# A graph network on one core: features before weights on one queue, digits of keys stored once, sixteen folded products ahead of the tail

## The reference

```
h = relu(layernorm(x));  x = x + attention(h, src, dst, W, a)         # softmax of scores over the edges of a node
h = relu(layernorm(x));  x = x + convolutions(h, [src,dst], W, b)     # three layers with self loops
h = relu(layernorm(x));  x = x + recurrent(h, [src,dst], W, GRU, MLP) # five steps
h = relu(layernorm(x));  x = x + weighted(h, src, dst, edge_weight, W1, b1, W2, b2)
```

## Time and profile before

| | us |
|---|---|
| median of 3 runs | 2409.83 |
| lowest and highest | 2408.52, 2412.48 |
| the profiled execution, whole | 2413.03 |
| its span (first to last instruction) | 2411.2 |
| prepare, until the barrier lets VectorE on | 105.8 |
| counts, until the scatter list is stored | about 199 |

### The profile page before, as it was taken

The page is one execution under the profiler, slowest core; times in us unless marked ns, Lnnn a source line. Parts: engine busy times, 40 slices in busy tenths (PEclk is TensorE's granted clock), DMA queues, the critical chain, the costliest instruction groups (busy, mean ns, idle before and its releaser), DMA issues.

```text
span 2411.2 us, 27684 instructions
## 1 busy us (share of the span) xinstructions
PE 2187.6 (91%) x9986; PEld 1206.7 (50%) x9987; DVE 1036.4 (43%) x2909; ACT 772.6 (32%) x1403; POOL 627.7 (26%) x434
## 2 busy tenths in 40 slices
PE   5599978998859996898999999999999999998998
PEld 4244467555525444354445554555445544464444
DVE  6699979998935457233112212122122111112202
ACT  3377767887823333222111111111111111112200
POOL 2000000000014433343444344443443344441000
PEclk9799955999979998899999999999999999999999
DMA  5200072444421112333222322223122322135582
GB/s 174 91 10 11 8 242 83 138 145 144 155 54 1 1 32 46 86 61 74 47 30 46 67 38 37 41 41 85 22 35 45 73 33 30 22 62 179 210 304 97
DMA packets 182305, 186.96 MB, mean 78 GB/s; under 512 B 105144, under 2 KB 168794, under 8 KB 178103
## 3 DMA queue, kind: packets, MB, share of 16 engines
q1 hardware_dynamic: 115288, 137.83, 18.2%
q0 software_dynamic: 56784, 1.28, 7.1%
q10 hardware_dynamic: 10106, 46.19, 5.3%
HBM read 100.85 MB, written 84.41 MB: 77 GB/s over the span
## 4 chain that ended last, share of the span: by engine, by line
PE 54%; DMA 3%; DVE 1%; issue 0%; ACT 0%; DVEq 0%; ACTq 0%
PE banks L1691 25%; PE banks L1716 21%; PE banks L1813 6%; DMA feat<-hnD 3%; PE banks L1769 1%; PE banks L1677 1%; PE banks L1778 0%; PE banks L1831 0%; DMA out_dram<-big 0%; DVE HN L1984 0%; DVE banks L1979 0%; ACT banks L1876 0%; DVE HN L1981 0%; PE banks L1828 0%; PE banks L1794 0%
## 5 line engine op out<-in xcount | busy, mean ns | idle before, releaser
L882 POOL DMA_INDIRECT WT<-lists x391 | 606.7, 1552 | 870.4 <-DMA WT<-lists 856.4
L1691 PE MATMUL banks<-big,feat 125*128 125x500 f16 (+1 forms) x3150 | 606.1, 353 | 19.7 <-DMA feat<-hnD 15.4
L1691 PEld LDWEIGHTS banks<-big,feat 125*128 125x128 f16 x3150 | 306.3, 97 | 309.7 <-DMA feat<-hnD 16.2
L1716 PE MATMUL banks<-H,U 128*128 128x500 f32 (+1 forms) x756 | 302.9, 541 | 8.4 <-issue 8.4
L1716 PE MATMUL banks<-aT,V 128*128 128x500 f32 (+1 forms) x756 | 296.4, 538 | 3.1 <-DVE HN L1984 3.1
L1716 PEld LDWEIGHTS banks<-aT,V 128*128 128x128 f32 x756 | 143.2, 190 | 145.2 <-issue 97.5
L1716 PEld LDWEIGHTS banks<-H,U 128*128 128x128 f32 x756 | 142.6, 191 | 138.1 <-issue 100.1
L1972 DVE SCALAR_TENSOR_TENSOR HN<-banks,bh,HN 128x500 f32<-128x500 f32 (+1 forms) x70 | 47.8, 682 | 376.6 <-ACT HN L1874 353.7
L1874 ACT ACTIVATE HN<-banks,bs 128x500 f32<-128x500 f32 (+1 forms) x70 | 44.4, 635 | 380.5 <-PE banks L1716 380.5
L1097 PE MATMUL banks<-work 125*128 125x500 f32 (+1 forms) x350 | 158.8, 568 | 7.6 <-DMA work<-xhD 5.2
L1334 PE MATMUL banks<-big,G 125*128 125x500 f16 (+1 forms) x700 | 142.8, 362 | 22.6 <-DVE G L1424 22.6
(11 more groups left out here) (299 smaller groups left out, 2282.2 us busy)
## 6 DMA issues: line engine op xcount, KB each, us to landing
big<-WT ACTq DMA_DIRECT2D x25, 1562.5 KB, 8.0
WT<-zero SPq DMA_DIRECT2D x39, 980.0 KB, 9.6
hTD<-HN SPq DMA_DIRECT2D x40, 250.0 KB
hnD<-stg SPq DMA_DIRECT2D x32, 250.0 KB
feat<-hnD SPq DMA_DIRECT2D x4, 2000.0 KB
H<-hTD SPq DMA_DIRECT2D x16, 500.0 KB
work<-xhD SPq DMA_DIRECT2D x28, 250.0 KB
WT<-lists POOLq DMA_INDIRECT x391, 3.0
```

Of the source, the lines that this page charges most:

```text
L882: nc.gpsimd.indirect_dma_start(out=WT, out_offset=bass.IndirectOffsetOnAxis(ap=lists[:, 0, t - first:t - first + 1], axis=0), in_=lists[:, ...
L1691: last = nc.tensor.matmul(SUMS[s % 2][half][:, 0:wid(ch)], rows_, A[:, j, cols(ch)], start=(j == 0 and part == 0), stop=(j == T - 1 and pa ...
L1716: last = nc.tensor.matmul(PS[bank][:, 0:w], wt_[:, kt, g:g + 128], v[:, kt, 0:w], start=(n == 0), stop=(n == len(terms) - 1))
```

## The change

1. **Loads.** The features `xn` move from ACT's queue to SP's, ahead of all weights and behind the edges. `acol` moves from POOL's queue to ACT's, and the store of `nearD` from SP's queue to ACT's, behind `acol`, with its wait for `EDGES`.
2. **Digits.** The product is now minus half the squared distance: rows 2 to 5 of `dig` are the integers, the same on both sides, rows 0 and 1 minus half the sum of squares in two parts. They are stored once, and rows 0 and 1 a second time as rows 6 and 7. A batch is loaded by two DMAs, rows 2 to 7 to partitions 2 to 7 of the one side, rows 0 to 5 to partitions 0 to 5 of the other; the two partitions left over on each side hold ones, which POOL writes once for all buffers at the start of `counts`, and SP waits for that (`ones_r`) before the first load. ScalarE computes Relu(1 + 2 p). VectorE no longer makes the multiples by -2, one cast and one difference; `UPPER` comes a step earlier, and POOL's two memsets in prepare go.
3. **Folded products.** `LATE` goes from 14 to 16: ten products instead of eight stand ahead of L422, and four instead of six in the tail (chunks 0 to 3).

```diff
@@ -62,7 +62,7 @@
-    digD = dram("digD", (EG * LANE, 8, 2, LANE), f16)
+    digD = dram("digD", (EG * LANE, 8, LANE), f16)
@@ -221,8 +221,8 @@
-        d0, d1, d2 = EG * 8 * LANE, EG * 12 * LANE, EG * 13 * LANE
-        dig = natural[:, 0:d0].bitcast(f16).rearrange("p (g k s e) -> p g k s e", g=EG, s=2, k=8)
+        d0, d1, d2 = EG * 3 * LANE, EG * 7 * LANE, EG * 8 * LANE
+        dig = natural[:, 0:d0].bitcast(f16).rearrange("p (g k e) -> p g k e", g=EG, k=6)
@@ -231,8 +231,8 @@
-        loaded, a_in, w_in, g_in, rest_in, eloaded, ew_in, padded, made, chain, ones_r = (
-            sem(s) for s in ("loaded", "a_in", "w_in", "g_in", "rest_in", "eloaded", "ew_in", "padded", "made", "chain", "ones_r"))
+        loaded, a_in, w_in, g_in, rest_in, eloaded, ew_in, padded, made, chain = (
+            sem(s) for s in ("loaded", "a_in", "w_in", "g_in", "rest_in", "eloaded", "ew_in", "padded", "made", "chain"))
@@ -255,7 +255,7 @@
-        EARLY, LATE = 6, 14
+        EARLY, LATE = 6, 16
@@ -281,7 +281,6 @@
-                pool.dma_start(acol[:], aA.rearrange("(h p) o -> p (h o)", p=128), allow_slow_non_contiguous=True).then_inc(a_in, 16)
@@ -318,9 +317,6 @@
-                pool.wait_ge(w_c, len(jobs))
-                g.memset(dig[:, :, 2:4, 0], 1.0)
-                g.memset(dig[:, :, 0:2, 1], 1.0).then_inc(ones_r, 1)
@@ -328,9 +324,8 @@
+                sp.dma_start(xn[:], x.rearrange("(k p) d -> p k d", p=P)).then_inc(x_in, 16)
-                sp.wait_ge(dve_did, EDGES)
-                sp.dma_start(nearD.rearrange("(g t e) o -> t g (e o)", g=EG, t=LANE), near1[:]).then_inc(cs_out, 16)
@@ -340,15 +335,15 @@
-                digits = digD.rearrange("(g t) k s e -> t g k (s e)", g=EG)
-                made_digits = dig[:].rearrange("t g k s e -> t g k (s e)")
+                digits = digD.rearrange("(g t) k e -> t g k e", g=EG)
-                sp.dma_start(digits[:, :, 4:8], made_digits[:, :, 4:8]).then_inc(outs, 16)
+                sp.dma_start(digits[:, :, 2:6], dig[:, :, 2:6]).then_inc(outs, 16)
-                sp.dma_start(digits[:, :, 0:4], made_digits[:, :, 0:4]).then_inc(outs, 16)
-                sp.wait_ge(outs, 16 * 7)
+                sp.dma_start(digits[:, :, 0:2], dig[:, :, 0:2]).then_inc(outs, 16)
+                sp.dma_start(digits[:, :, 6:8], dig[:, :, 0:2]).then_inc(outs, 16)
+                sp.wait_ge(outs, 16 * 8)
@@ -438,7 +433,7 @@
-                    if ch < SC - 1:
+                    if LATE + ch < VSTEPS:
@@ -448,7 +443,9 @@
-                act.dma_start(xn[:], x.rearrange("(k p) d -> p k d", p=P)).then_inc(x_in, 16)
+                act.dma_start(acol[:], aA.rearrange("(h p) o -> p (h o)", p=128), allow_slow_non_contiguous=True).then_inc(a_in, 16)
+                act.wait_ge(dve_did, EDGES)
+                act.dma_start(nearD.rearrange("(g t e) o -> t g (e o)", g=EG, t=LANE), near1[:]).then_inc(cs_out, 16)
@@ -652,22 +649,21 @@
-                digit = lambda s_, k: dig[:, :, k, s_, :]
-                ints = dig[:, :, 4:8, 1, :]
+                digit = lambda k: dig[:, :, k, :]
+                ints = dig[:, :, 2:6, :]
-                dve.wait_ge(ones_r, 1)
-                V_.tensor_scalar(digit(1, 4), cs[:, :, 1, :], -float(P // 2 + 1), None, ALU.add)
-                V_.tensor_scalar(digit(1, 6), tmp[:], -float(DIGIT // 2), None, ALU.add)
+                V_.tensor_scalar(digit(2), cs[:, :, 1, :], -float(P // 2 + 1), None, ALU.add)
+                V_.tensor_scalar(digit(4), tmp[:], -float(DIGIT // 2), None, ALU.add)
-                done(V_.tensor_scalar(digit(1, 7), tmp[:], -float(DIGIT // 2), None, ALU.add))
+                done(V_.tensor_scalar(digit(5), tmp[:], -float(DIGIT // 2), None, ALU.add))
-                done(V_.tensor_scalar(digit(1, 5), tmp[:], 1.0 / P, 1.0 / P - T // 2, ALU.mult, ALU.add))
+                V_.tensor_scalar(digit(3), tmp[:], 1.0 / P, 1.0 / P - T // 2, ALU.mult, ALU.add).then_inc(dve_did, 1)
+                dve.wait_ge(dve_did, UPPER)
-                V_.tensor_scalar(dig[:, :, 4:8, 0, :], ints, -2.0, None, ALU.mult).then_inc(dve_did, 1)
@@ -675,13 +671,11 @@
-                done(V_.tensor_scalar(tmp[:], tmp[:], -ROUND, 64.0, ALU.add, ALU.mult))
+                done(V_.tensor_scalar(tmp[:], tmp[:], -ROUND, -32.0, ALU.add, ALU.mult))
-                V_.tensor_copy(digit(0, 0), tmp[:])
-                V_.tensor_copy(digit(1, 2), tmp[:])
+                V_.tensor_copy(digit(0), tmp[:])
+                V_.scalar_tensor_tensor(digit(1), sq[:, :, 0], -0.5, tmp[:], ALU.mult, ALU.subtract).then_inc(dve_did, 1)
-                V_.tensor_tensor(digit(0, 1), sq[:, :, 0], tmp[:], ALU.subtract)
-                V_.tensor_tensor(digit(1, 3), sq[:, :, 0], tmp[:], ALU.subtract).then_inc(dve_did, 1)
@@ -708,6 +702,7 @@
+        ones_r = sem("w_ones")
@@ -733,16 +728,25 @@
+            @block.gpsimd
+            def _(pool):
+                nc.gpsimd.memset(dig[:], 1.0).then_inc(ones_r, 1)
+                def digits(b):
+                    tiles = slice(b * BATCH, (b + 1) * BATCH)
+                    for side, lo in enumerate((2, 0)):
+                        sp.dma_start(dig[lo:lo + 6, b % RD, :, side, :], digD[tiles, lo:lo + 6, :].rearrange("t k e -> k t e")).then_inc(d_in[b % RD], 16)
+                sp.wait_ge(ones_r, 1)
-                    sp.dma_start(dig[:, b].rearrange("k t s e -> k t (s e)"), digD[b * BATCH:(b + 1) * BATCH].rearrange("t k s e -> k t (s e)")).then_inc(d_in[b], 16)
+                    digits(b)
-                    sp.dma_start(dig[:, b % RD].rearrange("k t s e -> k t (s e)"), digD[b * BATCH:(b + 1) * BATCH].rearrange("t k s e -> k t (s e)")).then_inc(d_in[b % RD], 16)
+                    digits(b)
@@ -806,7 +810,7 @@
-                    nc.scalar.activation(eq[:, b % 2].rearrange("p t e -> p (t e)"), PS[2 + b % 2][:], ACT.Relu, bias=1.0, scale=-1.0).then_inc(eq_r, 1)
+                    nc.scalar.activation(eq[:, b % 2].rearrange("p t e -> p (t e)"), PS[2 + b % 2][:], ACT.Relu, bias=1.0, scale=2.0).then_inc(eq_r, 1)
@@ -818,7 +822,7 @@
-                    pe.wait_ge(d_in[b % RD], 16 * (b // RD) + 16)
+                    pe.wait_ge(d_in[b % RD], 32 * (b // RD) + 32)
```

More of the change, by code:

```diff
@@ L274, in prepare @@
         VSTEPS = 4 * GL
-        assert VSTEPS == LATE + SC - 1
+        assert VSTEPS <= LATE + SC - 1
         with nc.Block() as block:
```

## The result

The change makes the program **0.32% faster**: the ratio of the times is 0.9968, 95% interval 0.9958 to 0.9978. The changed kernel's median is 2402.87 us (2401.62 to 2405.52, 8 runs), that of the kernel before, measured beside it, 2410.80 us (2405.34 to 2417.72, 8 runs). That is 7.9 us where the forecast had 10.8 us. The time lies in the predicted range, 3.9 us above the number. The profiled execution took 2403.71 us with a span of 2401.8 us.

A forecast was written before the change was run, and what follows sets the result against it. The bound was a chain from features through VectorE's list, gathered keys, ScalarE's tail and the store of `h` to the barrier. Gains 6.1 + 1.7 + 0.5 + 1.9 + 0.6 = 10.8 us gave a 2399.0 us median, range 2392.5 to 2406.5.

The forecast's parts named there:

- counts gets longer: Sign of being wrong: the counts stage was to stay as long as before, 199.1 us to its end.
- Term 1: Prepare: features loaded first land at 22 to 23 us, so VectorE's list gains 12.4 us.
- Term 2: Prepare: later weights, `gW` about 30 us, make TensorE the late engine; the tail starts at 64.4 instead of 70.5, gaining 6.1 us.
- Term 3: ScalarE's tail: no wait for the first product saves 1.73 us, one product copy fewer saves 0.48 us.
- Term 4: Store of `h` to barrier: 1.9 us from the `VD` store no longer meeting it, 0.6 us from fewer digits.
- some 17 us for the store of `h`: Sign at the end of prepare: the prediction is wrong if this store does not take that long alone.
- Term 5: Counts: POOL's 2.9 us of writing ones and the paired digit loads are hidden and cost nothing.
- Rival 1: Prepare: `gW` lands at 26 us, 4 us more gained, 14.8 in all, total 2395 us; chance 0.14.
- Rival 2: Prepare: late weights (`gW` at 34) or TensorE's low clock leave a gain of 3.2 us, total 2406.6; chance 0.15.
- Rival 3: Counts: pairs of digit loads become the new wait, 62 us more less the 10.8, total 2461 us; chance 0.08.
- L559: Sign in prepare: this VectorE instruction, held by the features, starts at 22 to 24.5 us.
- the last early product: Sign in prepare: TensorE's final product ahead of the tail ends near 60 us.

The follow-up runs named there:

- rep_first: Changed kernel with the products of `rep` put ahead of the ten folded products; one run, barrier at 96.92 us, 0.7 us later than in the changed kernel.
- loads_alone: Kernel before with only the loads moved (part 1 of the change); median 2403.76 us, ratio 0.9970 to the kernel before.
- ones_early: Changed kernel with POOL writing the ones at the end of its list in prepare, not in counts; median 2403.83 us, ratio 0.9968 to the kernel before.
- late16_alone: Kernel before with only `LATE` raised from 14 to 16 (part 3); median 2410.76 us, ratio 0.9991 to the kernel before.
- digits_alone: Changed kernel with the loads and `LATE` put back, so only the digits changed; median 2411.94 us, ratio 0.9993 to the kernel before.
- ones_early_late14: Changed kernel with the ones written in prepare and `LATE` back at 14; median 2402.85 us, ratio 0.9964 to the kernel before.
- fill_in_counts: Kernel before plus six POOL memsets that nobody reads at the start of counts; one run, counts 200.1 us, 1.0 longer.
- x_split: Changed kernel with the load of features cut into 112 and 13 partitions; median 2394.79 us, ratio 0.9925 to the kernel before.

## Why the prediction was right, and which step failed

At the marks the gain is 3.6 us up to the tail, 2.2 within it and 3.9 from the store of `h` to the barrier, less 2.5 in counts: 7.1 us where the terms had 6.1, 2.2, 2.5 and 0. The time fell into the range, but two terms are off by 2.5 us each against the forecast and one by 1.4 in its favour, and one of the prediction's own signs of being wrong, that counts gets longer, came true.

**Term 1, features first: right in kind, the arrival 3 us late.** 22 to 23 forecast, 26.07 seen, so VectorE's list gained 9.7 us and not 12.4; the rate was that of the earlier trace rows, but the 1.5 us allowed for other transfers were too few. Which of them it was (the edges, the store of keys, or the weights that join from 21 us on) no run isolates. It costs nothing, as forecast, since VectorE had slack: it still waits 4.86 us at L627, and rep_first shows that wait to be free.

**Term 2, the weights come later: the late engine right, size off by 2.5 us.** TensorE did take VectorE's place, but not by the loads alone: loads_alone, with eight early products, has it late by 0.68 us, and there 8.7 of VectorE's 9.7 us stay. After, the two moved products (2.6 us) and slower transposes (2.1 us) lie on top. Of the 9.7 us 3.6 stay after, where the forecast kept 6.1 of 12.4. `gW` started at 31.86, not near 30: the working had let all loads run at weight rates behind 22 to 23, and the features ended 3 us later. The block took 30.8 us (31.86 to 62.65) instead of 29.9. Here executions differ: where the transposes ran at the full rate it took 28.8 (ones_early, 31.59 to 60.42, the end of its products), and the tail, 64.69, falls on the forecast 64.4 through two misses that cancel. Term 2's gain was 3.6 us after, 5.8 in ones_early, 6.1 forecast.

**Term 3, the tail: right.** From 66.91 to 79.60 are 12.69 us against 14.84, a gain of 2.15 where 2.21 was forecast.

**Term 4, store to barrier: 3.9 us instead of 2.5.** Of the 1.9 for the `VD` store and 0.6 for the digits, late16_alone shows 1.1 for the one and digits_alone 1.5 for the other; on the new loads the first is worth 2.5 (ones_early against ones_early_late14). The digits were undersized: I gave their half of the bytes 0.6, and the stretch shrank by more than the whole range of 0 to 1.3 allowed. The stretch of 16.65 us, digits included, does not contradict some 17 us for the store of `h`.

**Term 5, counts: the step that failed.** "POOL writes ones on 3072 columns; ... Hidden." priced the memset's length well (2.9 forecast, 2.65 seen) and its cover wrongly. It asked who waits for the memset: SP, with time to spare, and indeed SP's wait of 2.4 us for it is covered. It did not ask who works beside it. VectorE's comparisons are the pace of counts' start, and they stood still: 2.80 instead of 0.86 us. The Trainium skill ("SBUF — State Buffer", section "SBUF: two separate sides") calls the port pair that VectorE's two-port modes share with GpSimd an exclusive lock that one side holds for a whole instruction. By that rule comparisons that start at 96.71 stand until the memset ends at 98.86, at most 2.15 us (an estimate from the two rows); they lost 1.94, and the rows agree. The slowing itself is shown by ones_early and fill_in_counts; the port is the skill's reason for it, and no run here shows it. ones_early returns 2.3 to 3.0 us of counts by moving that one instruction. The 0.7 between 201.6 in after and 200.9 in the other kernels with the memset goes with the granted clock: it stays at 0.50 for 12 us behind the barrier in after, for 8 in digits_alone and x_split, for 4 in ones_early. No run isolates this.

**The rivals.** Rival 1 (`gW` at 26) fell because the eleven other engines did not run ahead. Rival 2 came in part: behind the wait for the weights the transposes of `gW` took 4.53 us, 2.1 more than in loads_alone and ones_early and 0.7 more than before. It looks like half clock, but the granted clock in these rows is 1.00. Before the tail the pace was up again. Rival 3 has fallen: the pairs of digit loads cost nothing that any row shows. TensorE has no wait for a DMA, and ones_early, with the pairs, has counts of 198.6 us, no more than the 199.1 of the kernel before.

Of the signs named, those on L559 (26.07 for 22 to 24.5), on the tail, on the last early product (ends at 62.65 for 60), on the store of `h` (79.60 for 77) and on counts failed, the last by the prediction's own word ("wrong ... if counts gets longer"); the waits gone at L417 and L426, no wait in the tail and the barrier near 95 held.

## What to carry to other kernels

Where a small instruction is added beside a busy stage, ask of it not only who waits for it but also who works beside it: here 2.65 us of POOL took 2 us from VectorE, and moving it into an idle stage gave them back in counts. Before reordering transfers, look at the share of the DMA engines that the large ones use: here a load on five of sixteen delayed the loads behind it on the queue, and cutting 125 partitions into 112 and 13 in two places (10.5 and 7.8 us at the barrier) was worth more than the whole reordering. And when a chain is shortened, price the chain next to it first: of the 9.7 us that VectorE gained 8.7 reached the tail in loads_alone, and 3.6 in the changed kernel, whose TensorE has two products more and ran its transposes slower.

## What the runs showed of the hardware

- **A load on few engines held the next issue on its queue.** The issue behind the 125-partition load lasted 17.61 us, though the share was that of five engines (0.38, 94 GB/s); split, both loads were issued in 5.81 us and the next began at 8.97. The Trainium skill ("DMA: Bandwidth & Descriptors", section "Why a DMA increments its semaphore by 16 and not by 1") gives the number of engines by the divisor rule, 16 for 112 partitions and 13 for 13; the split load's own stretch, 228 GB/s at a share of 0.92 from 6 to 8 us where the changed kernel has 163 at 0.56, agrees. It does not hold for every such transfer: behind the store of `h`, as large and also on 125 partitions, the digits' stores are issued in 0.37 and 2.31 us (83.67 and 84.09 after). The load is written as 125x25x128 and the store as 125x3200, so the number of pieces for each engine may be what counts; and in the kernel before the issue of `whh`, behind loads of 128 partitions and beside the features' load on ACT's queue, lasted 6.88 us too. No run separates the number of pieces from the number of engines.
- **A memset on 8 partitions holds up f16 comparisons on 128.** 2.80 us for three beside one memset of 2.65, 1.94 beside small ones, 0.86 without. Not every instruction of VectorE suffers: L761 (TENSOR_TENSOR), begun 0.04 us behind the same memset, took 0.55 us, as without it.
- **The same transposes take 2.4 or some 4 us.** The 20 transposes of `gW` took 2.40 or 2.41 us in three of the thirteen profiled executions (loads_alone, ones_early, fill_in_counts) and 3.86 to 4.53 in the other ten. After shows a granted clock of 1.00 from 28 to 36 us and took 4.53. Whether the record misses a spell of the clock or the cause is another, no run shows; a difference of 2 us at TensorE needs this row read beside it.
